# Expert weights loaded one per tile over the whole last attention instead of two per tile over its first half

## What is computed

```
x = x + latent cross attention(layernorm(x), ctx)          # fourth
x = x + grouped attention(layernorm(x), Wq, Wk, Wv, bias)  # fifth: 16 heads of 16, 4 key/value groups, causal, 32 x 32
h = layernorm(x)                                           # sixth: mixture of 8 experts, one per token
e = argmax(sigmoid(h @ router_w)); p = its value
x = x + p * ((silu(h @ gate_w[e]) * (h @ up_w[e])) @ down_w[e])
```

## Time and profile before

| | |
|---|---|
| three timed runs | 1162.98, 1167.76, 1168.69 us, median 1167.76 |
| the profiled execution's own time | 1165.53 us |
| its span, first to last instruction | 1163.8 us |
| mean granted TensorE clock | 0.982 of full |
| TensorE busy (matmul) | 1100.2 us, 95% of the span |
| VectorE, ScalarE, GpSimd busy | 703.4, 469.4, 305.2 us |
| last attention, span time | about 894 to 1012 us |
| all DMA queues in 890 to 1000 us | 13.41 MB, of which 8.39 MB are the 16 expert loads |

### The profile page before, as it was taken

One profiled execution on the slowest core, in us unless ns is written; L12 is line 12 of the kernel. 1 busy time (PEld: TensorE's weight loads), 2 busy tenths in 40 slices (PEclk: granted clock), 3 DMA queues, 4 the chain that ended last, 5 costly groups with the idle time before them and its releaser, 6 DMA issues. The chain is left out here.

```text
span 1163.8 us, 32560 instructions
## 1 busy us (share of the span) xinstructions
PE 1100.2 (95%) x12594; PEld 850.1 (73%) x12595; DVE 703.4 (60%) x1802; ACT 469.4 (40%) x1361; POOL 305.2 (26%) x408
## 2 busy tenths in 40 slices
PE   7898999999999899999979999999998799899996
PEld 5676887787888678898766777777775688556664
DVE  6897646464554575554548888888885587522221
ACT  2453444352534312121155555655652466322221
POOL 1701000000000000000153645546533554434442
PEclk9899999999999999999999999999999999899999
DMA  8631000000000036000101110211114843312210
GB/s 253 187 84 34 1 1 1 0 0 0 0 0 0 1 73 202 1 0 1 38 10 38 50 56 28 54 48 34 56 30 170 230 109 78 112 28 35 36 27 11
DMA packets 60205, 61.57 MB, mean 53 GB/s; under 512 B 26862, under 2 KB 51087, under 8 KB 59628
## 3 DMA queue, kind: packets, MB, share of 16 engines
q1 hardware_dynamic: 51836, 41.35, 13.3%
q0 software_dynamic: 8304, 19.32, 6.4%
HBM read 52.33 MB, written 10.14 MB: 54 GB/s over the span
## 5 line engine op out<-in xcount | busy, mean ns | idle before, releaser
L1730 ACT ACTIVATE xattn_exps<-xattn_ps_s,xattn_top 128x256 f32<-128x256 f32 x256 | 117.8, 474 | 77.7 <-DVE xattn_top L1798 77.7
L766 PEld LDWEIGHTS attn_ps_q<-attn_xnT,w_b_q 128*128 128x128 f32 x1024 | 120.9, 196 | 12.6 <-issue 12.6
L766 PE MATMUL attn_ps_q<-attn_xnT,w_b_q 128*128 128x128 f32 x1024 | 125.5, 279 | 0.0
L1256 POOL TENSOR_TENSOR fold_last_cos<-raw_last,all_consts 64x64 f32<-64x64 f32 x1 | 0.3, 312 | 456.4 <-POOLq L1064 456.4
L820 PE MATMUL attn_ps_out<-w_b_o,attn_oT 128*128 128x256 f32 x480 | 106.5, 380 | 1.8 <-DVE all_x L1001 1.5
L820 PEld LDWEIGHTS attn_ps_out<-w_b_o,attn_oT 128*128 128x128 f32 x480 | 90.0, 190 | 15.0 <-DVE all_x L1001 2.4
L874 ACT COPY attn_qT<-attn_ps_q 128x512 f32<-128x512 f32 x64 | 38.1, 595 | 150.2 <-PE attn_ps_q L766 150.2
L1805 DVE STREAM_TRANSPOSE xattn_expsT<-xattn_exps 128x1024 f32<-128x1024 f32 x64 | 79.4, 1241 | 21.2 <-ACT xattn_exps L1730 21.2
L1795 DVE TENSOR_REDUCE xattn_raw_top<-xattn_ps_s 128x4 f32<-128x1024 f32 x64 | 77.8, 1216 | 13.5 <-PE xattn_ps_s L1622 13.4
L1622 PE MATMUL xattn_ps_s<-xattn_kT,xattn_qT 64*32 64x256 f32 x2048 | 69.5, 381 | 2.9 <-ACT xattn_exps L1730 2.9
L1632 PE MATMUL xattn_ps_o<-xattn_expsT,xattn_kv 32*64 32x256 f32 x2048 | 63.5, 381 | 4.7 <-DVE xattn_last_scores L1841 4.0
(11 more groups left out here) (361 smaller groups left out, 2324.4 us busy)
## 6 DMA issues: line engine op xcount, KB each, us to landing
xattn_inverse<-xattn_inverse_rows SPq DMA_DIRECT2D x30, 256.0 KB, 3.8
all_c<-in_ctx SPq DMA_DIRECT2D x64, 64.0 KB, 1.9
moe_gate<-in_f_gate SPq DMA_DIRECT2D x8, 512.0 KB, 8.5
moe_up<-in_f_up POOLq DMA_DIRECT2D x8, 512.0 KB, 5.5
moe_down<-in_f_down POOLq DMA_DIRECT2D x8, 512.0 KB, 5.3
xattn_v_stage<-xattn_v_rows SPq DMA_DIRECT2D x16, 136.0 KB, 2.1
xattn_v_blocks<-xattn_v_stage SPq DMA_DIRECT2D x64, 34.0 KB, 2.0
attn_v_blocks<-attn_v_stage SPq DMA_DIRECT2D x64, 34.0 KB, 1.9
```

Source lines behind the costliest of these rows:

```text
L766: last = nc.tensor.matmul(ps_q[g % 2][:, h * P:(h + 1) * P], wq[:, c, head * DH:(head + 1) * DH], xnT[u][:, c, :], start=(c == 0), stop=(c ...
L1730: nc.scalar.activation(exps[g % 2][:, nkeys * k:nkeys * (k + 1)], ps_s[g % 2][:, nkeys * k:nkeys * (k + 1)], ACT.Exp, bias=top[u][:, n:n + ...
```

## The change

In GpSimd's loop, t runs from 1 to 18. Before, the first eight passes issue two loads each; now passes 3 to 18 issue one each. It is the same 16 DMAs in the same order.

```
             for t in range(1, TILES + POOL_LEAD - 1):
                 if t < TILES:
                     normalise(t)
-                if t <= EXPERTS:
-                    next(loads)
+                if t > 2:
                     next(loads)
                 if t == 3:
                     g.iota(count_rows[:, :], [[1, P]], 0, 0).then_inc(s["counted"], 1)
```

## The result

The changed kernel takes 1175.11 us (median of 4 runs, 1173.51 to 1177.58) against 1166.14 us for the kernel before: ratio 1.008, 95% interval 1.0045 to 1.0115, slower by 0.8%. Measured again over 12 runs, its median is 1169.64 and the ratio 1.001 (0.9984 to 1.0035); runs over 1.5% above the fastest of their kernel count as slow and are left out of ratios, here three at about 1183 us, with which the mean of the 12 would be 0.5% above that of the kernel before. The two intervals don't overlap, so how much slower the change is stays open between nothing and 0.8%; neither shows the forecast gain. The forecast was 1161.0 with a range of 1157.0 to 1166.5, and both medians lie above it.

What follows compares the result with a forecast made beforehand. TensorE, busy for 95% of the span, was taken to bound the kernel. Head -6.14 us, middle nothing, tail +0.6 made -5.5: 1160.0 from the profiled run, 1162.2 from the median, so 1161.0 us, range 1157.0 to 1166.5.

Steps and rivals of the forecast that it cites:

- What bounds the kernel, and the head: Attention steps 2 to 4: TensorE's waits behind paired loads and late tables mostly go, a gain of 6.14 us.
- Moved into the middle: nothing: Passes 5 to 14: one load in each stays under the cover of TensorE's step and costs nothing.
- The sign that the prediction set against itself: In the profile after, a middle step above 5 us or a wait over 2 us ahead of any weigh would refute it.
- Moved to the tail: a cost of 0.6 us: Last tiles: loads of passes 15 to 17 delay stage(14), making weigh(14) and weigh(15) late; 0 to 2.2 us, taken as 0.6.
- Slower: the tail becomes the new head: Rival, chance 0.08: stage(14) and stage(15) each cost 6.93 us, the clock 1 us more; 10.0 against 6.14, so 1169.4.
- the head's jitter: Rival, chance 0.14: the median run's extra 2.2 us is the head's stall and goes too; gain 8.4, so 1159.4.

Runs made afterwards that it cites:

- h_nudge: Changed kernel with the last four loads behind the last addition, plus stage(4) held until normalise(6) is done; first gather 119.2 us after normalise(0).
- a_tail_out: Changed kernel with the loads of passes 15 to 18 issued after the last addition; 1167.02 us, ratio 0.998 to the kernel before.
- d_filler: Changed kernel with four idle 512-column products on TensorE just ahead of weigh(14); 1168.43 us, ratio 0.999 to the kernel before.
- g_skip4: Changed kernel without the load of pass 4 and with five loads after the last addition; 1159.72 us, ratio 0.994 to the kernel before.
- t_tail_back: g_skip4 with the loads of passes 15 to 18 back in place, one load left after the last addition; 1164.86 us, ratio 1.000.
- g_nudge: g_skip4 with stage(4) held once until GpSimd has normalised tile 6; first gather 110.7 us after normalise(0).
- g_hold: g_skip4 with stage(4) held once until GpSimd has added tile 2; step 15 at 86.5 us after normalise(0), first gather at 115.9.
- b_head_only: Kernel before with loads moved: none in passes 1 and 2, one each in 3 and 4, two each in 5 to 11; ratio 0.999.
- before again: The kernel before, unedited, with a second profile; first gather 115.9 us after normalise(0).
- c_none_inside: Changed kernel with all 16 loads issued after the early rows, none inside the attention; 1183.37 us.
- c_hold: c_none_inside with stage(4) held once until GpSimd has added tile 2; step 15 at 81.2 us after normalise(0), first gather at 129.5.
- g_again: g_skip4 unedited, measured and profiled again; 1159.25 us, ratio 0.996 to the kernel before.
- chg_look_1: The changed kernel, unedited, with a further profile; first gather 123.2 us after normalise(0).
- chg_look_2: The changed kernel, unedited, with another further profile; whole time 1182.16 us, first gather 124.5 us after normalise(0).

## Why the prediction was wrong

**What bounds the kernel, and the head: right.** Step 5 was forecast 6.14 us earlier. It came 5.7 us earlier after `normalise(0)` (33.3 against 39.0), step 2 with 6.02 us against 5.99 forecast, stage(2) with 3.68 us under the 4 forecast, no wait ahead of weigh(1) and weigh(2), full clock. Beside one load a stage takes 1.7 to 2.4 us more than the 1.54 alone, as much as or more than the 1.7 us for which the whole load holds the engines. The Trainium skill's "DMA: Bandwidth & Descriptors", section "Queues, rings and completion order", says that a DMA engine takes turns between its queues a whole packet at a time, typically 9 to 17 descriptors. I had read that as turns within a load. A load is 144 packets in the profile's count (2304 for the 16 in the earlier trace rows), 9 for each of the 16 engines. If what the profile counts are that section's descriptors, a whole load can be one turn, and that would fit stage(2), of which 6 packets moved beside 103 of the load's and 138 behind them. No run here tests this reading.

**"Moved into the middle: nothing": this step failed.** It priced a load by TensorE's step from 933.57, which ran at 4.81 us beside a pair. That step showed that blocks(t) had room to be late, not that SyncE's path kept up. Nor does a DMA engine that is free for two thirds of the step help: in the steps that lost time the engines were busy for 0.44 to 0.52 of it. SyncE's rows of the kernel before already had the price, beside the pairs of 934.22 and 939.03, and they weren't read:

```profile
937.75 0.34 SPq L2004 DMA_DIRECT2D attn_v_stage<-attn_v_rows  x1
941.46 1.73 SPq L2008 DMA_DIRECT2D attn_v_blocks<-attn_v_stage  x4
943.29 0.38 SPq L2004 DMA_DIRECT2D attn_v_stage<-attn_v_rows  x1
946.81 1.73 SPq L2008 DMA_DIRECT2D attn_v_blocks<-attn_v_stage  x4
```

Stage(6) takes 3.71 us and stage(7) 3.52, and rounds last 5.5 and 5.4 us. The sum that was missing is SyncE's own round: stage plus 1.73 us of issues plus 0.1, against 4.85. With a stage of 2.0 it is 3.8 and fits; with 3.5 it is 5.3 and doesn't. Before, only two pairs were issued after the long wait of step 3, and from pass 9 on there was nothing to keep a late stage late. With a load in every pass it stayed late to pass 14 in four profiles of six (the three of the changed kernel and h_nudge, not a_tail_out and d_filler): in the changed kernel step 15 starts at 87.2 to 87.8 where it did at 87.1 to 87.5 before. There the middle gives back all that the head gives. A path that is on time has its stage out 1.3 us ahead of the load (g_skip4); it wasn't looked at what happens to one that is late, though stage(2) was forecast at 4.04 us, 2.5 over its price alone, in the same text. The sign that the prediction set against itself, a step of the middle above 5 us, came eight times, and so did the other, a wait of over 2 us ahead of a weigh, once.

**"Moved to the tail: a cost of 0.6 us": mis-sized, and a term was left out.** The mechanism was seen: three loads close together, stage(14) among them. Stage(14)'s price, taken as 3.4 to 4.04 us, was 4.36; one of blocks(14) took 1.67 us to issue, as one had taken 1.53 before (the 2.83 us of the earlier trace rows), and I had counted 1.74 for all four. Stage(14) also starts 0.07 us after its step does, where it was 0.72 us ahead before, since the middle left SyncE late. Together weigh(14) waited 3.95 us against at most 1.4. What I priced only in the rival, at 1 us, was the clock: from weigh(14) to the last logits, among the router's small products, it is 20.6 us instead of 13.3. The other two profiles of the changed kernel have 15.8 and 19.9 us behind waits of 3.90 and 1.11, t_tail_back 20.4 behind 1.48. The two profiles of before have 13.3 and 12.5 there.

**The rivals.** "Slower: the tail becomes the new head", at 0.08, had the sign and the place, with 1169.4. Its point of decision was wrong: it asked for two stages at 6.93 us, where one at 4.36 and the clock were enough. None of the rivals was in the middle.

**The size.** Counted from `normalise(0)` to the end, the three profiles of the changed kernel take 275.9, 271.7 and 276.1 us, the two of before 269.3 and 264.6: 7.6 us more on average, 0.65%, between the two measured ratios; the profiles of one kernel differ by up to 4.7 us, so the size is rough. The spread between runs that I took for the head's jitter is in good part older than the attention: its start alone varies by 10.7 us. Why a_tail_out and d_filler ran quick and h_nudge slow, with the same loads in the middle, is settled only in part. In a_tail_out stage(3) went out 0.23 us behind a load's issue and took 2.68 us, and stage(4), 0.09 behind, took 1.83 and was on time. In d_filler and h_nudge stage(3) went out 0.50 and 0.47 us behind and took 4.11 and 3.94, and weigh(3) waited 1.57 and 1.43 us. In d_filler the clock then fell to 0.73 (step 5 takes 6.24 us), which put off the next load: stage(6) went out 0.87 us ahead of it and took 1.61. In h_nudge the clock stayed at 1.00 (5.05 us), and stage(6) went out 0.94 us behind the load and took 3.86. Why the clock fell in the one and not in the other stays open. g_nudge and g_hold bracket what decides: 0.1 us behind a load's issue is worked off, 1.6 us isn't.

## What to carry to other kernels

Before spreading transfers evenly over a loop, add up the round of each serial path that shares the DMA engines (here SyncE's store, wait and read back) with the price that it pays beside a transfer, and compare it with the loop's step. If it is longer, one late round can last as long as the transfers do. Leave the passes free of them in which the path is late anyway, here the one just ahead of stage(2), and the burst ahead of the last tiles. Price a wait on TensorE with the clock behind it, above all where small products follow.

## What the runs showed of the hardware that was not expected

- A store of 34 KB that goes out 1.0 to 1.8 us after the issue of a single 512 KB load takes 3.3 to 4.0 us to land (2.91 for the held one of g_hold; more in the bursts of the tail); 0.15 to 0.7 us after it 2.7 to 4.1; 0.1 us after it 1.79 (g_nudge) and 1.83 (a_tail_out); 1.2 to 1.4 us ahead of it, and so 3.4 us or more behind the load before, 1.9 to 2.6; with no load near 1.5 to 1.7 as a rule. Its packets come behind nearly all of the load's when they fall due among them.
- Near the last tiles SyncE loses 0.5 to 1.8 us once, in fourteen of the sixteen profiles, loads or not: either the issues of blocks(14) or blocks(15) take 2.2 to 3.1 us instead of 1.73 (before, b_head_only, g_skip4, g_nudge, h_nudge, g_hold and all three profiles of the changed kernel) or stage(15) takes 3.05 to 3.3 us with nothing beside it (before again, c_none_inside, c_hold, a_tail_out, g_again). The cause isn't shown. In the changed kernel it is part of weigh(14)'s wait.
- A single wait of 1.48 us on TensorE, ahead of small products, was followed by 20 us at 1.2 GHz up to the last logits (t_tail_back), where the same products after no wait had 6.7 (g_skip4) and 1.6 (g_again).
- The granted clock, averaged over the first 10 us behind the first gather, comes out at three values, and the rest of the span goes with it. It is 1.00 in the changed kernel, chg_look_1, d_filler, g_nudge and before again, with a rest of 148.5 to 148.7 us; 0.83 in b_head_only, h_nudge, g_skip4, g_again, t_tail_back and g_hold, with 150.1 to 150.4; 0.66 in before, chg_look_2 and a_tail_out, with 151.6. (The two kernels whose gather came late, c_none_inside and c_hold, have 0.64 and 0.60 with 150.2 and 150.6.) chg_look_1 and chg_look_2 are the same code: 3 us of their whole times go with this alone.
